# Graph attention stage: logits from a broadcast row of targets and a leaky relu in place of score products, the mask laid once a sample, and eight heads' sums by TensorE

## The reference, cut to what matters

```
h = x @ W[head]                      # 256 x 32
th = tanh(h)
attn = th @ w_src + (th @ w_dst).T   # 256 sources x 256 targets
attn = where(attn >= 0, attn, 0.2 * attn)
attn = where(~adj, -999.0, attn)
attn = softmax(attn, axis=-1)
out = elu(concat over heads(attn @ h + b))
gate = sigmoid(x @ H_w.T + H_b)
result = gate * out + (1 - gate) * x
```

## Time and profile before

| | us |
|---|---|
| median of 3 runs | 2715.39 |
| lowest and highest | 2708.66, 2715.69 |
| the profiled execution | 2709.26 |
| its span, first to last instruction | 2707.5 |

### The profile page before, as it was taken

How to read it: one execution, slowest core, us unless ns; L and a number is a source line. 1 busy time by engine, 2 the same in 40 slices (tenths; PEclk the granted TensorE clock), 3 DMA queues, 4 the chain that set the end, 5 groups by cost and what they waited for, 6 DMA issues and landing times. The chain is left out here.

```text
span 2707.5 us, 66704 instructions
## 1 busy us (share of the span) xinstructions
PE 2640.9 (98%) x20128; PEld 2385.9 (88%) x20128; DVE 2417.2 (89%) x7209; ACT 2346.9 (87%) x6600; POOL 1804.9 (67%) x1550
## 2 busy tenths in 40 slices
PE   8999999999998999999999999999999999999996
PEld 7888888888887999999999999899999999999995
DVE  6998998898887999999999999899999999999995
ACT  7999999999998888888888888888888888888884
POOL 3777766766765677766666677766666666667665
PEclk9999999999999999999999999999999999999998
DMA  3011111111104888887778888878778887878775
GB/s 99 28 38 40 33 34 39 33 33 39 37 29 130 256 260 259 263 253 252 247 252 255 256 262 264 252 255 251 253 242 259 256 250 254 253 245 257 250 249 176
DMA packets 386754, 500.42 MB, mean 185 GB/s; under 512 B 58464, under 2 KB 349152, under 8 KB 386272
## 3 DMA queue, kind: packets, MB, share of 16 engines
q1 hardware_dynamic: 386400, 496.16, 58.2%
HBM read 219.24 MB, written 201.33 MB: 155 GB/s over the span
## 5 line engine op out<-in xcount | busy, mean ns | idle before, releaser
L794 ACT ACTIVATE probs<-logits,nmax 128x256 f32<-128x256 f32 x1152 | 571.8, 500 | 104.5 <-DVE turned_sb L1072 99.6
L570 POOL TENSOR_TENSOR probs<-probs,recs 128x1024 f32<-128x1024 f32 x288 | 545.9, 1896 | 107.8 <-DVE recs L1064 107.6
L1072 DVE STREAM_TRANSPOSE turned_sb<-probs 128x512 f32<-128x512 f32 x576 | 610.7, 1103 | 4.0 <-POOL probs L570 4.0
L1051 DVE CUSTOM_DVE_ANT_0 logits<-s,mask 128x256 f32<-128x256 f32 x1152 | 430.8, 420 | 84.1 <-PE s L1456 81.4
L548 POOL TENSOR_TENSOR residual<-x,br 128x384 f32<-128x384 f32 x192 | 191.0, 1017 | 455.9 <-DVE mix L1083 455.8
L787 ACT ACTIVATE stack<-split 64x768 fp32r<-64x768 f32 x576 | 484.8, 842 | 3.4
L76 PE MATMUL pj<-xt_hi,w_lo 128*128 128x256 f32 x1728 | 481.9, 279 | 0.8 <-DVE xt_lo L1036 0.8
L78 PE MATMUL pj<-xt_hi,w_hi 128*128 128x256 f32 x1728 | 481.0, 278 | 0.0
L77 PE MATMUL pj<-xt_lo,w_hi 128*128 128x256 f32 x1728 | 480.8, 278 | 0.0
L665 ACT ACTIVATE g_exps<-g_v,g_nmax 128x256 f32<-128x256 f32 x768 | 385.3, 515 | 3.0 <-DVE g_nmax L961 0.7
L779 ACT ACTIVATE split<-pj,bc 128x256 fp32r<-128x256 f32 x576 | 239.6, 467 | 163.2 <-PE pj L78 107.3
(11 more groups left out here) (118 smaller groups left out, 7401.3 us busy)
## 6 DMA issues: line engine op xcount, KB each, us to landing
turned<-turned_sb SPq DMA_DIRECT2D x288, 512.0 KB, 5.0
pt_copy<-turned SPq DMA_DIRECT2D x288, 512.0 KB, 4.6
stack<-split SPq DMA_DIRECT2D x576, 128.0 KB, 4.4
y<-out SPq DMA_DIRECT2D x128, 384.0 KB, 5.2
x<-y SPq DMA_DIRECT2D x96, 384.0 KB, 3.1
x<-x SPq DMA_DIRECT2D x32, 384.0 KB, 3.0
adj<-adj SPq DMA_DIRECT2D x128, 64.0 KB, 3.1
w_whole<-att_w SPq DMA_DIRECT2D x24, 192.0 KB, 2.9
```

What stands on the lines that cost most here:

```text
L570: pool.tensor_tensor(probs[:, heads, :, :].rearrange("p h t n -> p (h t) n"), probs[:, heads, :, :].rearrange("p h t n -> p (h t) n"), rec ...
L794: last = act.activation(probs[:, (HEADS * u + h) % 4, t, :], logits[:, h % 2, t, :], ACT.Exp, scale=-1.0, bias=nmax[:, u, h, t:t + 1], acc ...
L1051: last = dve.tensor_tensor_reduce(out=logits[:, h % 2, t, :], in0=s_ps[h % 2][:, t, :], in1=mask[u][:, t, :], scale=-HEAD_DIM ** -0.5, sca ...
L1072: last = dve.transpose(turned_sb[b][:, :, :].rearrange("p k (z h q) -> p k z h q", z=NT, h=2 * NT)[:, :, kt], probs[:, 2 * b:2 * b + 2, :, ...
```

## The change

It touches the graph stage and its crossing alone.

- Logits. The score products and the spread of targets on GpSimd are gone. The sd product is one plain fp32 product for each chunk instead of three fp32r ones, from a copy of the transposed tanh that isn't split. ScalarE copies its PSUM result once with a per-partition sign (`g_rows_of_sd`). SP writes the 12 rows of targets to DRAM and reads them back broadcast to 128 partitions, in three DMAs of four heads. VectorE turns the source rows to columns by four transposes (`g_turn_rows`). ScalarE then makes the logit of a half with one Prelu instruction: the targets' row is the input, the source's number the bias, so two instructions a head.
- Mask. TensorE lays it into PSUM once a sample, in `s_ps[u]` (`g_lay_mask`). VectorE's maximum adds it to the logits.
- Sums. The exps of heads 0 to 7 have no accumulator. TensorE makes their sums by 16 further products with columns of ones, of the contexts' shape, into the other half of the context's PSUM tile. The first two context copies stay as they were, the third takes both halves; one more transpose a half brings the sums back, and VectorE inverts them from PSUM (`g_invert_sums`). Heads 8 to 11 keep the accumulator.
- Other engines. The elu and the gating go from VectorE to GpSimd. Evictions of transposed exponentials: ScalarE keeps pairs 1, 3 and 5 of the even heads, VectorE has the rest.
- Order. The slot now has the samples nxt, cur, prev, old and done in flight. The last three heads of a sample are finished in the next slot, and the elu of a sample comes one slot later than before. The lists of all engines and the crossing are written anew.

```diff
-            def g_relu(half, u, h):
-                act.wait_ge(g_scores, at(GAT_HEADS, half, u, h + 1))
-                act.wait_ge(g_exped, at(GAT_HEADS, half, u, h - 2))
-                act.activation(g_v_sb[:, h % 3], s_ps[h % 2][:, :, :], ACT.Relu, scale=-0.8).then_inc(g_lrelu, 1)
+            def g_leaky(half, u, h):
+                g_targets_ready(act, half, u, h)
+                for t in range(NT):
+                    last = act.activation(g_v_sb[:, h % g_V_BUFS, t, :], g_targets[u][:, h, :], ACT.Prelu, scale=-1.0,
+                                          bias=g_source[u][:, t, h:h + 1], alpha=LEAKY)
+                last.then_inc(g_leaky_done, 1)
...
+                    if g_summed_on_pe(h):
+                        last = act.activation(out, logits_of, ACT.Exp, scale=-1.0, bias=bias)
+                    else:
+                        last = act.activation(out, logits_of, ACT.Exp, scale=-1.0, bias=bias, accum_out=g_sums[:, u, h, t:t + 1])
...
+            def g_targets_ready(eng, half, u, h):
+                eng.wait_ge(g_targets_spread[u][h * g_PARTS // GAT_HEADS], 16 * (half + 1))
+                eng.wait_ge(g_sources_turned, at(1, half, u, 1))
+                eng.wait_ge(g_exped, earlier(GAT_HEADS, half, u, h + 1 - g_V_BUFS))
...
+            def g_lay_rows(half, u):
+                held(sp, g_rows_ready, at(1, half, u, 1), passed)
+                sp.dma_start(targets_dram[u], g_rows[g_TARGETS, :]).then_inc(g_rows_laid, 16)
+            def g_spread(half, u, i):
+                sp.wait_ge(g_rows_laid, 16 * (2 * half + u + 1))
+                held(sp, g_leaky_done, earlier(GAT_HEADS, half, u, -GAT_HEADS), passed)
...
+            def g_slot(far, nxt, cur, prev, old, done):     # SP
+                if cur:
+                    g_spread(*cur, 1)
+                    g_spread(*cur, 2)
+                if done:
+                    g_store(*done)
+                if far:
+                    g_load_next(*far)
+                if nxt:
+                    g_lay_rows(*nxt)
+                    g_spread(*nxt, 0)
...
+            def g_elu(half, u):                             # GpSimd
+                pool.wait_ge(g_ctx_exp, at(1, half, u, 1))
+                pool.tensor_scalar(g_cx[:, :, :], g_cx[:, :, :], 0.0, None, ALU.max).then_inc(g_elu_parts, 1)
+                pool.tensor_scalar(g_ce[:, :, :], g_ce[:, :, :], -1.0, None, ALU.add).then_inc(g_elu_parts, 1)
+                pool.wait_ge(g_elu_parts, at(2, half, u, 2))
+                pool.tensor_tensor(g_cx[:, :, :], g_cx[:, :, :], g_ce[:, :, :], ALU.add).then_inc(g_elu_done, 1)
+            def g_gated_elu(half, u):
+                pool.wait_ge(g_x_used, at(1, half, u, 1))
+                pool.tensor_scalar(g_gate[u][:, :, :], g_gate[u][:, :, :], 1.0, None, ALU.add).then_inc(g_gate_more, 1)
...
+                pool.tensor_tensor(mix[:, :, :], g_gate[u][:, :, :], g_cx[:, :, :], ALU.mult).then_inc(g_gated, 1)
...
+            def g_lay_mask(half, u):                        # TensorE
+                pe.wait_ge(g_mask_ready, at(1, half, u, 1))
+                pe.wait_ge(g_maxed, earlier(GAT_HEADS, half, u, -GAT_HEADS))
+                pe.matmul(s_ps[u][:, :, :], g_ident_r[:, :], g_mask[u][:, :, :], start=True, stop=True).then_inc(g_mask_laid, 1)
```

More of the change, by code:

```diff
@@ L41, in f32, with g_every_slot, sample @@
     return ap.bitcast(F32)
[L44 to L50, removed]
+def g_every_slot(slot):
+    def sample(k):
+        return divmod(k, 2) if 0 <= k < B else None
+    for k in range(B):
+        slot(sample(k + 1), sample(k), sample(k - 1), sample(k - 2), sample(k - 3), sample(k - 4))
 def every_slot_of_all_layers(slot, behind=3):
@@ new lines, in g_copy_state, with g_turn_rows @@
+            def g_copy_state(half, u, t):
+                dve.wait_ge(g_state_turned, at(NT, half, u, t + 1))
+                dve.tensor_copy(g_tt[:, :, t * P:(t + 1) * P], pj_ps[g_TT_BANK[t]][:, 0:D].rearrange("p (c n) -> p c n", c=DC)).then_inc(g_tt_ready, 1)
+            def g_turn_rows(half, u):
+                dve.wait_ge(g_rows_ready, at(1, half, u, 1))
+                for q in range(BLOCKS):
+                    rows = slice(q * BLOCK, (q + 1) * BLOCK)
+                    last = dve.transpose(g_source[u][rows, :, :], g_rows[rows, :].rearrange("p (t q n) -> p t q n", t=NT, q=BLOCKS)[:, :, q, :])
+                last.then_inc(g_sources_turned, 1)
@@ L1195, in _ @@
             dve.wait_ge(g_ident_loaded, 16)
-            dve.tensor_copy(g_ident_r[:, :], ident[:, :])
-            for p in range(2):
-                for part, rows in ((g_z_left, g_DST), (g_s_dst, g_SRC)):
-                    last = dve.tensor_scalar(part[p][rows, :], ident[rows, 0:1].to_broadcast([g_HALF, N]), 0.0, 1.0, ALU.mult, ALU.add)
-            last.then_inc(g_consts_ready, 1)
+            dve.tensor_copy(g_ident_r[:, :], ident[:, :]).then_inc(g_consts_ready, 1)
             dve.wait_ge(g_w_hi_done, 2)
@@ L1306, in g_four_contexts @@
                 pe.wait_ge(g_ctx_read, at(g_GROUPS, half, u, g))
+                ones = g_sel[:, 1 + g * GAT_DIM:1 + (g + 1) * GAT_DIM] if g < g_ON_PE else None
+                if g == 1:
+                    for kt in range(NT):
+                        for i in range(g_QUAD):
+                            pe.matmul(cx_ps[i * GAT_DIM:(i + 1) * GAT_DIM, N:2 * N], ones, g_pt_sb[:, g_pt_slot(u, first + i), kt, :], start=False, stop=kt == NT - 1)
                 for kt in range(NT):
@@ L1312, in g_four_contexts, with g_slot @@
                                          start=kt == 0, stop=kt == NT - 1)
+                if g == 0:
+                    for kt in range(NT):
+                        for i in range(g_QUAD):
+                            last = pe.matmul(cx_ps[i * GAT_DIM:(i + 1) * GAT_DIM, N:2 * N], ones, g_pt_sb[:, g_pt_slot(u, first + i), kt, :], start=kt == 0, stop=False)
                 last.then_inc(g_contexts, 1)
[L1315 removed]
+            def g_slot(far, nxt, cur, prev, old, done):
                 if nxt:
                     g_transpose_x(*nxt, 0)
+                if prev:
+                    g_pair_of_transposes(*prev, 3)
                 if cur:
[L1319 to L1320 removed]
+                    g_make_gate(*cur, 1)
+                if prev:
+                    g_pair_of_transposes(*prev, 4)
                 if nxt:
```

868 lines of the change are left out of this document (423 added, 445 removed).

## The result

| us | before | after |
|---|---|---|
| median | 2714.64 | 2846.08 |
| lowest to highest, runs | 2708.66 to 2715.69, 4 | 2840.73 to 2850.61, 4 |
| span of the profiled execution | 2707.5 | 2846.3 |

The ratio is 1.0489, 95% interval 1.0469 to 1.0508. The forecast had the direction and a seventh of the size: +20 against +131, far outside its range.

What follows compares the result with a forecast made beforehand. ScalarE was taken as the graph stage's floor, 25.6 us a sample after the change, period 25.9. 2709.3 + 19 (longer period) + 2 (fill) + 5 (crossing) = 2735 us, range 2700 to 2768.

Steps and rivals of the forecast that it cites:

- ScalarE's sum, 25.6 us: Graph stage: ScalarE's instructions after the change total 25.6 us a sample, 1.4 more than before, and set the floor.
- four tensor_scalars of 768 columns at 0.83: Graph stage, GpSimd: elu and gating, with two tensor_tensors at 1.85, add 7.0 us; GpSimd 19.5 us a sample.
- It has room, and its chain ends before VectorE comes to its statistics: Graph stage: GpSimd's elu, gating and total take 8.0 us from ScalarE's slot end, finishing before VectorE's statistics.
- VectorE and TensorE: Graph stage: VectorE falls to 21 us a sample, four small transposes costing 0.8; TensorE falls to 17 to 20.
- The DRAM trip: Graph stage: targets' row through DRAM takes 8.5 to 9.8 us, fitting ScalarE's 10.5 us before the next leaky relu.
- rival B: Graph stage: DRAM trip late or TensorE-to-ScalarE waits unchanged; period 26.9 to 27.2, total 2765 to 2785; chance 0.14.
- Rival C: Graph stage, ScalarE: leaky relu and plain exp cost 0.36, floor 24.0, period 24.4, total 2688; chance 0.14.
- The fill: Start of the graph stage: first sample waits for two DMAs, +2 us (0 to +6).
- The crossing: Between graph and attention stages: GpSimd's last elu, gating and total precede normalise(first, 1); +5 us (-8 to +8).

Runs made afterwards that it cites:

- e6: e5 plus, in the slots, GpSimd's adds in two-operation form, the gate's addition before the wait, three even evictions moved from ScalarE to VectorE; 2706.76 us, ratio 0.9978.
- e1: Changed kernel with GpSimd's four single-operation tensor_scalars of 768 columns (min, max, two adds) written in two-operation form; 2768.80 us, ratio 1.0211.
- e9: e6 with an unused 3872-byte tile, so the attention stage's moved tiles have before's addresses again; 2697.68 us, ratio 0.9942.
- e10: Kernel before with its tiles from w_whole0 to w_lo1 3872 bytes lower, at the changed kernels' addresses; 2722.34 us, ratio 1.0036.
- e5: Changed kernel with the crossing's three elus and gatings on VectorE and normalise(first, 1) ahead of the last total; 2837.68 us, ratio 1.0459.
- e8: e6 with the first attention sample's projections and splits drawn earlier in the crossing's order; 2715.98 us, ratio 1.0015.
- e2: Changed kernel with the gate's addition on GpSimd moved ahead of the wait for elu's exp in the slots; 2788.98 us, ratio 1.0284.
- e11: e6 with the tiles from w_whole0 to w_lo1 32 bytes higher, w_hi0 at 76384; 2698.45 us, ratio 0.9949.
- e12: e9 with its gap 32 bytes longer, w_hi0 at 80256; 2694.49 us, ratio 0.9934.

## Why the prediction was wrong, step by step

- **ScalarE's sum, 25.6 us: right.** 0.40 for a leaky relu, 0.40 and 0.49 for the exps, all seen; after's period less ScalarE's waits is 25.7. e6 shows the sum as the bound where nothing waits. In after it wasn't the bound: 28.56.
- **GpSimd, "four tensor_scalars of 768 columns at 0.83": the step that failed.** They take 2.14. GpSimd was to be at 19.5 us a sample; 5.2 more makes 24.7, and after has 23.7 from 300 to 700 us (331.40 busy in 14.0 samples). The row was of the right engine, shape and name, and of another pair of operations. For the leaky relu, which had no row, the prediction bounded the cost from both sides; here it took a row as if it were of the operation and gave no bounds. The tensor_tensors at 1.85 were right.
- **"It has room, and its chain ends before VectorE comes to its statistics": failed too.** The chain was reckoned at 8.0 us against one reader. It is 10.1 from the exp to the gate's release, and with the total 12. The reader missed was ScalarE, whose gate tanh waits for the same chain in the next slot. The change itself put a slower engine between two ScalarE instructions. At 0.83 us the three tensor_scalars in the chain would have ended it 3.9 us sooner, at 509.4 in the rows above, before ScalarE reaches the gate at 511.1: the price made the wait, by way of a reader that nobody had listed, and no rival had it. ScalarE's 25.6, 2.35 at the gate and 0.47 at TensorE's product L82 make 28.4 of the 28.56.
- **VectorE and TensorE: right as covers, wrong in TensorE's size.** The small transposes took 235 ns, 0.94 for the four against 0.8; VectorE has 20.6 us a sample against 21. TensorE fell to 82% in after, but that is 23.5 us a sample, and 22.2 in e1 at a clock of 1.00, against the forecast's 17 to 20: durations that overlap were subtracted from a busy time that counts an overlap once. That its granted clock would fall to 0.91 or 0.93 was not foreseen; e1 has 1.00. What the lower clock cost in after was not separated. ScalarE's 0.47 us a sample for TensorE's product, which e1 doesn't have, bounds what reached ScalarE's list directly.
- **The DRAM trip (rival B): it fits, as forecast.** In after it is 1.5 us from the write's issue to the spread's (495.40 to 496.86), then 5.5: 7 against 8.5 to 9.8. Rival C's 0.36 didn't appear.
- **The fill: +1.7 against +2.** Right.
- **The crossing: +5 against +35.** Of the 35.1: about 12 is the place of the tiles (e9, e10), no part of any step; 10 is GpSimd's chain with normalise's place (e5), which the forecast had, at too low a price; about 13 stays open. 11 of it lies between the last exp and the first transpose, 12.1 us in before and 23.1 in e9. e8 tried the order of the first attention sample and made it worse.

Together, of the 139 us: 101 are the longer period. ScalarE's sum of 25.6 alone would have made it 10, (25.6 - 25.29) x 31; the wait at the gate is 73 (2.35 x 31), the one for TensorE's product 15 (0.47 x 31), and 3 are not placed. 12 are the memory map, 10 GpSimd in the crossing, 13 open, the rest the fill and the seams. That the forecast had the direction is in part luck: the sum it reasoned from carries 10 us, under a tenth of the loss.

## What to carry to other kernels

A row prices an instruction only with its operations: before work moves to an engine, find a row with the same operation there, or keep a range. When a step moves to a slower engine, list everything that waits for its result, the next round's writers of its inputs included, and add up the circle as well as the engines' sums: e2 gained 57 us by moving one instruction out of such a circle. And a change that adds or removes a tile moves all tiles behind it; if a stage nobody touched gets slower, put them back before explaining it.

## What the runs showed of the hardware

- GpSimd tensor_scalar, 128x768 fp32: multiply then add 0.83 us; a single add, min or max 2.14; multiply then min or max 2.79. The Trainium skill (GPSIMD Engine Reference, "Engine selection") calls one-input operations roughly line-rate; by estimate, at a column a cycle and that page's 1.2 GHz, that is 0.64 us for 768 columns. Multiply-add comes near it with 0.83, the other pairs don't.
- 128x256 fp32r products take 278 to 279 ns at w_hi0's byte 80224 or 76384, 280 at 80256, 281 to 283 at 76352, at a granted clock of 1.00: 12 us over 1850 in the profiled executions, 8 to 12 in the medians. e9, e11 and e12 scatter by 4 us among themselves (1830.9 to 1834.8).
- 32x64 STREAM_TRANSPOSE on VectorE: 235 ns, where an estimate by columns from the 128x512 one (1.10 us) gives 0.14.
